# Four graph layers on one core: probabilities turned through scratch memory, columns spread by TensorE, one low part moved to GpSimd

## The reference

```python
def layer0(x):   # scores from two products
    e = leaky_relu((x @ W1) @ (x @ W2).T, 0.2)
    return relu(softmax(where(adj > 0, e, -inf)) @ (x @ W3))

def gat(x, W, a, masked):   # layer 1 is elu(...) of this, masked
    h = x @ W
    e = leaky_relu((h @ a1)[:, None] + (h @ a2)[None, :], 0.2)
    return softmax(where(adj > 0, e, -inf) if masked else e) @ h

def layer2(x):   # the "mixed" layer
    o = relu(x @ mlp1 + b1)                             # 512 wide
    o = elu(elu(gat(relu(o), W_fc, a_fc, False))) + o
    o = relu(o @ mlp2 + b2)                             # 256 wide
    return relu(elu(elu(gat(o, W_hand, a_hand, True))) + o)

def layer3(x):   # masked attention, 4 heads of 64, output product with wo
    ...
```

## Time and profile before

| | |
|---|---|
| median of 3 runs | 2919.27 us (2908.69 to 2920.22) |
| the profiled execution | 2918.28 us, its span 2916.5 us |
| TensorE busy | 2689.4 us, 92% |
| VectorE, ScalarE, GpSimd busy | 2278.2, 1998.7, 1556.0 us |
| mean granted TensorE clock | 0.983 of full speed |
| DMA | 195.17 MB, mean 67 GB/s |

### The profile page before, as it was taken

One profiled execution on the slowest core, in us unless ns is written; L12 is line 12 of the kernel. 1 busy time (PEld: TensorE's weight loads), 2 busy tenths in 40 slices (PEclk: granted clock), 3 DMA queues, 4 the chain that ended last, 5 costly groups with the idle time before them and its releaser, 6 DMA issues.

```text
span 2916.5 us, 61536 instructions
## 1 busy us (share of the span) xinstructions
PE 2689.4 (92%) x22472; PEld 2551.3 (87%) x22472; DVE 2278.2 (78%) x6124; ACT 1998.7 (69%) x4801; POOL 1556.0 (53%) x2119
## 2 busy tenths in 40 slices
PE   4689999999999999999999999999999999999974
PEld 4589999999999999998999998999999999998863
DVE  3257888888888888888888887888888888888874
ACT  1357777777777776777777777777777777776752
POOL 0235555555555555555556555555655555555542
PEclk9799999999999999999999999999999999999997
DMA  3001222222122122212212221221222122122222
GB/s 109 19 16 37 77 81 64 57 81 80 41 80 81 59 63 80 74 47 81 80 51 71 81 72 49 81 81 48 74 81 70 52 80 80 41 81 73 66 66 73
DMA packets 132766, 195.17 MB, mean 67 GB/s; under 512 B 14832, under 2 KB 97136, under 8 KB 132464
## 3 DMA queue, kind: packets, MB, share of 16 engines
q1 hardware_dynamic: 132464, 191.24, 22.7%
HBM read 107.30 MB, written 83.89 MB: 66 GB/s over the span
## 4 chain that ended last, share of the span: by engine, by line
PE 60%; DMA 13%; ACT 8%; SPq 8%; DVE 6%; issue 4%; POOL 1%; POOLq 0%; DVEq 0%
PE ps L224 29%; DMA p4T<-scratch 10%; PE ps L378 6%; SPq L208 6%; PE ps L240 5%; PE ps L436 4%; PE ps L337 4%; PE ps L233 3%; PE ps L338 3%; DMA scratch<-p 3%; DVE p L950 3%; PE ps L456 2%; ACT p L671 2%; PE ps L360 2%; DVE h_lo L692 1%
## 5 line engine op out<-in xcount | busy, mean ns | idle before, releaser
L1067 POOL TENSOR_TENSOR p<-p,rd 128x512 f32<-128x512 f32 x256 | 269.8, 1054 | 20.0
L671 ACT ACTIVATE p<-p,nmx 128x256 f32<-128x256 f32 x512 | 255.7, 504 | 25.4 <-DVE nmx L935 25.2
L991 POOL TENSOR_TENSOR o1Tp_lo<-o1T,o1Tp_hi 128x1024 fp32r<-128x1024 f32 x64 | 153.8, 2403 | 220.8 <-ACT o1Tp_hi L472 220.8
L1003 POOL TENSOR_SCALAR xn<-act,nmean,rstd 128x256 f32<-128x256 f32 x384 | 243.6, 643 | 18.3 <-POOL rstd L998 11.2
L456 PE MATMUL ps<-p4T,v 128*64 128x256 f32 x1024 | 144.3, 404 | 118.2 <-DMA p4T<-scratch 117.7
L995 POOL TENSOR_TENSOR vare<-mv,eps 128x2 f32<-128x2 f32 x256 | 108.0, 422 | 270.5 <-DVE mv L748 270.5
L1060 POOL TENSOR_TENSOR rd<-some,den 128x2 f32<-128x2 f32 x256 | 53.5, 209 | 354.6 <-DVE den L944 354.6
L456 PEld LDWEIGHTS ps<-p4T,v 128*64 128x64 f32 x1024 | 67.3, 140 | 178.1 <-DMA p4T<-scratch 96.5
L692 DVE TENSOR_TENSOR xnT_lo<-ps,xnT_hi 128x512 fp32r<-128x512 f32 x192 | 132.1, 688 | 114.2 <-ACT xnT_hi L472 114.2
L935 DVE CUSTOM_DVE_ANT_0 p<-ps,mask 128x256 f32<-128x256 f32 x512 | 189.9, 418 | 33.3 <-PE ps L436 33.3
L480 ACT ACTIVATE sco<-sco,nmax 128x256 f32<-128x256 f32 x384 | 191.0, 500 | 28.9 <-DVE nmax L736 28.9
(11 more groups left out here) (248 smaller groups left out, 12683.1 us busy)
## 6 DMA issues: line engine op xcount, KB each, us to landing
scratch<-p SPq DMA_DIRECT2D x128, 512.0 KB, 2.9
p4T<-scratch SPq DMA_DIRECT2D x512, 128.0 KB, 3.9
x0T<-in_xT SPq DMA_DIRECT2D x64, 256.0 KB, 4.6
x<-in_x SPq DMA_DIRECT2D x64, 256.0 KB, 3.7
out<-xn SPq DMA_DIRECT2D x64, 256.0 KB, 3.0
o1T<-in_mlp SPq DMA_DIRECT2D x1, 512.0 KB, 4.4
p<-in_mlp SPq DMA_DIRECT2D x1, 512.0 KB, 4.5
att<-in_fc SPq DMA_DIRECT2D x1, 512.0 KB, 5.4
```

The lines of the kernel that those rows point to most:

```text
L671: ins = nc.scalar.activation(rows_, rows_, ACT.Exp, scale=-1.0, bias=nmx4[:, h, m:m + 1], accum_out=den4[:, h, m:m + 1])
L991: return G.tensor_tensor(lo, whole, hi.bitcast(fp32), ALU.subtract)
L1003: ins = G.tensor_scalar(xn[:, m, :], y[:, m, :], nmean[i][:, m:m + 1], rstd[i][:, m:m + 1], ALU.add, ALU.mult)
L1067: G.tensor_tensor(rows_, rows_, rd4[:, h, :].unsqueeze(2).unsqueeze(3).broadcast_to([P, NT, QUADS, CT * QP]), ALU.mult).then_inc(S["p4n"], 1)
```

## The change

- The probabilities of layers 0, 1 and the mixed layer no longer pass through TensorE (`t0`, `t1`, `t3` of TensorE are gone). VectorE turns 32x32 blocks from `sco` into `act` (`turn`), SP sends them to scratch (`o0 o1 o3`) and fetches them back into `sco` (`i0 i1 i3`), ScalarE makes the high part from there and GpSimd the low part (`t0 t1 t3` of its string). The mixed layer's `o3T`, which is added to the output, goes the same way (`o5`, `i5`, buffer `o3r`) in place of TensorE's `o3`.
- The column sums of the mixed layer's first attention come from four products of 256 columns with a 128x128 tile of ones, so that every partition holds them. VectorE makes the reciprocal of 128x256 from PSUM straight into `rdb`; `b2` on TensorE and its copy are gone.
- The low part of `o2T` (the input of `mlp2`) is made by GpSimd (`z2`) and no longer by VectorE; so is the last layer's norm (`n4`).
- Scores of layers 1 and 2 are written to `sco` in SBUF and no longer in place in PSUM, `ef` to `pfc`. Layer 0's product with the probabilities has bank 2, layer 1's bank 3; `enter` now guards each bank by itself. `xnT` has two buffers for three uses, `xn3` one; `x0T` lies in the place of its own low part, `pfc` too.
- Weights are loaded and split in four groups. Only the first (with `adj`) stands ahead of the first sample; `before` in `run` puts the rest of the set-up ahead of the steps that need it.
- All five order strings are new.

```diff
-    "sp": "lt:0 o40:7 st:9 o42:7 lx:1 i40:7 i42:7",
+    "sp": "i42:8 o5:6 o1:3 lt:0 i1:3 o0:1 i5:6 o3:6 st:8 i0:1 i3:6 o40:7 lx:1 o42:7 i40:7",
-    "pe": "h3:8 a0:3 v4:9 f3:8 x0:5 g0:2 s40:9 d2:7 x1:6 t3:8 s42:9 v2:7 a3:8 m2:6 h0:2 b2:7 n2:6 o3:8 w2:7 s0:2 h1:5 c2:6 f1:5 t0:2 a4:9 r2:6 t1:5 x3:8 y4:9 m3:7 n3:7 a1:5 f2:6 q4:8 k4:8",
+    "pe": "g0:0 c2:4 a1:3 h1:2 r2:4 a3:6 a0:1 f2:4 f1:2 a4:7 m3:5 y4:7 x1:3 h0:0 x3:6 m2:3 s0:0 q4:6 k4:6 h3:5 n2:3 v4:6 f3:5 d2:4 s40:6 v2:4 w2:4 s42:6 x0:1",
+    "ac": "h0:1 x3:7 p1:3 x2:5 q4:7 m2:4 s0:1 k4:7 h3:6 p0:1 n2:4 l0:0 u3:6 o2:4 p3:6 p40:7 t1:3 p41:7 y2:5 x0:2 p42:7 p43:7 k2:5 c2:4 a1:3 t0:1 t3:6 h1:2 z2:5 r2:4 a3:6 b3:6 g0:0 a0:1 u1:2 a4:7 f2:4 m3:5 o3:5 x1:3 w2:4",
+    "dv": "e3:6 s40:7 s41:7 t3:6 p40:7 v2:5 s42:7 p41:7 s43:7 n2:5 x0:2 p42:7 i2:5 p43:7 x40:7 c2:4 x42:7 b1:3 j2:5 a1:3 h1:2 i3:6 r2:4 c3:6 st1:3 i0:1 b3:6 a3:6 ag1:3 r3:6 f2:4 z3:6 a4:7 st3:6 ag3:6 g0:0 b2:4 y4:7 o3:5 x1:3 e1:2 h0:0 x3:6 st4:7 st0:1 ag4:7 t1:2 ag0:1 i1:2 q4:6 e0:0 k4:6 h3:5 t0:0 v4:6 d2:4",
+    "po": "v0:2 n4:8 w2:5 n0:2 l0:0 m2:4 d40:7 t1:3 p40:7 d41:7 p41:7 d42:7 p42:7 d43:7 p43:7 k4:7 t3:6 t0:1 y1:3 z2:5 v1:3 n1:3 v3:6 n3:6 a0:1 m3:5 v4:7",
...
+            def pro_out(i):
+
+                def step(t):
+                    sp.wait_ge(S[f"pro{i}_x"], t + 1)
+                    wait(sp, S[f"pro{i}_dma"], back(t - 1))
+                    sp.dma_start(scratch_pro[i].rearrange("p w n -> p (w n)"), flat(act[i])).then_inc(S[f"pro{i}_dma"], 16)
+                return step
+
+            def pro_in(i):
+
+                def step(t):
+                    sp.wait_ge(S[f"pro{i}_dma"], sent(t))
+                    rows_ = sco[i][:, :, :, :].rearrange("p b a n -> p (b a n)").rearrange("p (q n) -> p q n", q=QUADS)
+                    for w in range(QUADS):
+                        sp.dma_start(rows_[w * QP:(w + 1) * QP, :, :], scratch_pro[i][:, w, :].rearrange("(q j) n -> j q n", q=QUADS)).then_inc(S[f"pro{i}_dma"], 16)
+                return step
...
             def d2(t):
+
                 pe.wait_ge(S["pfcl"], t + 1)
-                for m in range(NT):
-                    for k in range(NT):
-                        for i in (1, 0):
-                            ins = nc.tensor.matmul(ps[:, 5, 2 * m:2 * m + 2], pfcp[i][:, k, m * P:(m + 1) * P], ones2[:, :],
-                                                   start=(k == 0 and i == 1), stop=(k == NT - 1 and i == 0))
+                enter(5, "rdb", t + 1)
+                for k in range(NT):
+                    for i in (1, 0):
+                        ins = nc.tensor.matmul(ps[:, 5, 0:N], ones2[:, :], pfcp[i][:, k, :], start=(k == 0 and i == 1), stop=(k == NT - 1 and i == 0))
                 ins.then_inc(S["d2_mm"], 1)
...
             def d2(t):
                 dv.wait_ge(S["d2_mm"], t + 1)
-                V.reciprocal(rdc[:, :], ps[:, 5, 0:4:2]).then_inc(S["rdc"], 1)
+                wait(dv, S["att"], t)
+                V.reciprocal(rdb[:, :], ps[:, 5, 0:N]).then_inc(S["rdb"], 1)
...
+            def turn(i):
+
+                blocks = sco[i][:, :, :, :].rearrange("p b a n -> p (b a) n").rearrange("p c (w j) -> p w c j", w=QUADS)
+                return V.transpose(flat(act[i]).rearrange("p (w c j) -> p w c j", w=QUADS, j=QP), blocks)
...
             def t0(t):
-                dv.wait_ge(S["proT0h"], t + 1)
-                low_part(proT[0], bank[0]).then_inc(S["proT0"], 1)
+                dv.wait_ge(S["pro0"], t + 1)
+                wait(dv, S["xn0"], t)
+                turn(0).then_inc(S["pro0_x"], 1)
...
+            def z2(t):
+                po.wait_ge(S["o2Th"], t + 1)
+                low_part(o2T[1][:, :, :], att[:, :, :], o2T[0][:, :, :]).then_inc(S["o2T"], 1)
...
+            def low_of_turned(pair, i):
+                source = sco[i][:, :, :, :].rearrange("p b a n -> p (b a n)").rearrange("p (q c i) -> p c q i", q=QUADS, i=QP)
+                lo, hi = (flat(h).rearrange("p (c q i) -> p c q i", q=QUADS, i=QP) for h in (pair[1], pair[0]))
+                return low_part(lo, source, hi)
```

More of the change, by code:

```diff
@@ L18, in parse, with run @@
     return [(name, int(stage)) for name, stage in (x.split(":") for x in text.split())]
-def run(engine, steps, B):
+def run(engine, steps, B, before={}):
     order = parse(ORDERS[engine])
@@ L27, in run @@
             if 0 <= k - s < B:
+                if k == s and name in before:
+                    before[name]()
                 steps[name](k - s)
@@ L163, in by_quads, with by_tiles, flat, sent @@
             return row.rearrange("p (b w j) -> p w b j", b=CT, w=QUADS)
+        def by_tiles(row):
+            return row.rearrange("p (b n) -> p b n", b=CT)
+        def flat(tile):
+            return tile[:, :, :].rearrange("p a n -> p (a n)")
+        def sent(t, n=QUADS):
+            return 16 * (n + 1) * t + 16
+        def back(t, n=QUADS):
+            return 16 * (n + 1) * (t + 1)
         def wait(eng, sem, n):
@@ L375, in mlp2 @@
[L375 to L380 removed]
+                pe.wait_ge(S["pfcl"], t + 1)
+                enter(5, "att", t + 1)
+                product3(half_of(5), hfc, pfcp, NT, 2, off=2).then_inc(S["w2_mm"], 1)
@@ L475, in leaky, with high_of_turned, graph_scores, renew @@
                 return nc.scalar.activation(dst, src, ACT.Prelu, bias=bias, alpha=SLOPE)
+            def high_of_turned(pair, i):
+                source = sco[i][:, :, :, :].rearrange("p b a n -> p (b a n)").rearrange("p (q c i) -> p c q i", q=QUADS, i=QP)
+                return copy(flat(pair[0]).rearrange("p (c q i) -> p c q i", q=QUADS, i=QP), source)
             def exps(i):
                 for m in range(NT):
-                    ins = nc.scalar.activation(sco[i][:, m, :], sco[i][:, m, :], ACT.Exp, scale=-1.0, bias=nmax[i][:, m:m + 1], accum_out=den[i][:, m:m + 1])
+                    ins = nc.scalar.activation(sco[i][:, :, m, :], sco[i][:, :, m, :], ACT.Exp, scale=-1.0, bias=nmax[i][:, m:m + 1], accum_out=den[i][:, m:m + 1])
                 return ins
-            def graph_scores(b, i):
-                leaky(ps[:, b, N:2 * N], ps[:, b, 0:N], cols[i][:, 0, 0:1])
-                return leaky(ps[:, b, 0:N], ps[:, b, 0:N], cols[i][:, 1, 0:1])
-            ac.wait_ge(S["made"], 1)
+            def graph_scores(tile, i):
+                for m in range(NT):
+                    ins = leaky(tile[:, :, m, :], by_tiles(ps[:, 1, 0:N]), cols[i][:, m, 0:1])
+                return ins
+            readers = []
+            def renew(read, n):
+                if readers:
+                    ac.wait_ge(S[readers[0]], readers[1])
+                readers[:] = [read, n]
             def l0(t):
@@ L718, in _, with split @@
-            dv.wait_ge(S["setup_pool"], 1)
-            V.tensor_copy(ones2[:, :], ones[:, :])
+            count = {"wsplit": 0}
+            def split(places):
+                for pair, rows_, cols_, whole in places:
+                    ins = V.tensor_copy(pair[0][:, rows_, cols_], whole)
+                ins.then_inc(S["wsplit"], 1)
+                count["wsplit"] += 1
+                dv.wait_ge(S["wsplit"], count["wsplit"])
+                for pair, rows_, cols_, whole in places:
+                    ins = V.tensor_tensor(pair[1][:, rows_, cols_], whole, pair[0][:, rows_, cols_].bitcast(fp32), ALU.subtract)
+                return ins
@@ L895, in r3 @@
             def r3(t):
-                dv.wait_ge(S["on3_mm"], t + 1)
+                dv.wait_ge(S["o3_dma"], back(t))
                 dv.wait_ge(S["q3"], t + 1)
-                V.tensor_tensor(act[2][:, :, :], act[2][:, :, :], bank[2], ALU.add).then_inc(S["r3"], 1)
+                for m in range(NT):
+                    row = act[2][:, m, :].rearrange("p (k q c) -> p k q c", k=CT, q=QUADS)
+                    ins = V.tensor_tensor(row, row, o3r[:, :, :, m, :].rearrange("p q k c -> p k q c"), ALU.add)
+                ins.then_inc(S["r3"], 1)
             def z3(t):
```

518 lines of the change are left out of this document (292 added, 226 removed), and 3 rows, old and new, of the table ORDERS.

## The result

The changed kernel takes 3025.04 us (median of 4 runs, 3024.26 to 3029.68) against 2916.61 us of the kernel before on the same chip: ratio 1.0362, 95% interval 1.0335 to 1.0389. It is slower; the forecast was 2817 us, faster, with a range that ended at 2910.

What follows compares the result with a forecast made beforehand. The round was taken as a loop of PE segment A plus stretch L, 23.4 + 17.9 = 41.3 us. Then 245 + 63 x 41.3 - 47 + 15 = 2815, with 1.8 around it 2817 us; range 2690 to 2910.

Steps and rivals of the forecast that it cites:

- PE's work: TensorE's work a round: 41.05 us less 2.48 for removed turns, spread and cheaper `d2`, so 38.6.
- L: Stretch from the end of `s42` until `p4T` is there for `a4`: 18.6 us before, forecast 17.9.
- A: PE segment from second half of `a4` to end of `s42`, without a gap: 24.1 us before, forecast 23.4.
- the line on the masks of layers 1 and 2: VectorE's masks reading scores from SBUF: extra cost between nothing and 0.97 us each, taken as 0.
- The reciprocal: VectorE's pass over 128x256 from PSUM: taken at 0.45 us, between 0.43 and 1.4.
- slack on PE is 0.8 us: Claim that `s40` on PE, with `d2` running just ahead of its masks, has 0.8 us to spare.
- The rival: VectorE and GpSimd block each other, adding 1.0 in L and 2.0 in A: round 44.3, 3004 us; chance 13%.
- the forecast's own signs: Forecast wrong if PE waits inside A, POOL or SP queue chain shares rise well, or two-source passes grow 0.5 each.
- DVE's sum: VectorE's busy time a round: 35.19 us before, forecast 34.2, hidden below the round of 41.3.
- Start and end: Ramp and drain: first product at 13 us instead of 45.16, `a4` first passing at 245, end 15 after last `a4`.
- The drain: End of the run: saves 47 us against full rounds, as in the kernel before, and stays so.
- The sum: Whole time: 245 + 63 x 41.3 - 47 + 15 = 2815, with 1.8 us around the span 2817.

Runs made afterwards that it cites:

- all cures: Changed kernel plus scores of layers 1 and 2 in PSUM, `z2` on VectorE, `o1Tp_lo` in halves, `a1` ahead of `j2`: 2841.45 us, ratio 0.9758.
- e3: Not a run: a step in VectorE's string, two masks over 128x256, ahead of `s40` and `s41`; no time of a kernel belongs to it.
- The swap: `a1` put ahead of `j2` in VectorE's string: 2854.24 us on PSUM scores with wide reciprocal; 2900.46 against 2925.81 with the old column sums.

## Why the prediction was wrong, step by step

- **PE's work, right.** 38.6 a round forecast, 39.03 measured.
- **L, right in its sum, by luck in its parts.** From the end of `s42` (1469.74) to the second half of `a4` (about 1486.9, which no longer waited) it is at most 17.2; forecast 17.9. `a3`'s wait of 1.78 for VectorE lies in it, so the path through `p4T` is not what set it there. With all cures, where `p4T` is waited for, L is 17.6. But `x42` ends 9.0 after `s42` in the changed kernel and 8.8 with all cures (1435.6), not 7.9 to 8.2: GpSimd's last product with the reciprocals ends at 7.7 (1477.47) and not 6.7, and its small step `rd` over 128x2 takes 0.54 on average and up to 1.18, 0.21 before, as in the meetings with VectorE. And from there to `p4T` it takes 8.8, not the 9.7 that were to stay, since the DMA out took 3.29 and not 3.94, the last one in 4.18 and not 4.40. Two errors of nearly a microsecond cancel. SP's 20 more issues did not delay `o42` or `i42` beyond that: the three issues between out and in still take 1.3 us.
- **A, wrong, and with it the sign.** Forecast 23.4; measured 27.2 (1442.5 to 1469.74). PE's waits inside it in this round are 0.54 (`m3`), 1.00 (`s0`), 0.29 (`s40` for `v`) and 1.83 (`s42`), 3.7 together. The forecast had none of them. With all cures 0.46 (for `nmax`) and 0.30 (`s40` for `v`) are left, and A is 24.2.
- **The step that failed** is the line on the masks of layers 1 and 2: "lower bound unchanged, upper 0.97 more for each", and "I take 0, since PE doesn't wait on them now". The measured cost is 0.79 for each, four a round. That PE did not wait on them in the kernel before said nothing of the new string, in which they stand between two products of PE: `e1` ahead of `h0` and `s0`, `e3` ahead of the masks for which `s42` waits. The upper bound (0.97) was near the mark; taking the lower one was the error. The run with the scores in PSUM gave 5.2% back, more than the whole 3.6% of loss.
- **The reciprocal, mis-sized.** Taken at 0.45 with an upper bound of 1.4; measured 1.757, outside the bound. The bound came from the difference of two rows with two elements a partition (0.15 and 0.14), too small a difference to give the time of an element. With "slack on PE is 0.8 us" this is 1.3 us of work over 0.8 of slack. It is shown by the run without the division: 4.6%. With the masks cured it costs 0.4 to 0.6% (2864.93 to 2852.29, 2841.45 to 2828.95).
- **Both together.** One loop explains why the two did not add. `d2` on PE, the reciprocal, `e3`'s masks, those of `s40` and `s41`, `s42`: either cure takes `s42`'s wait of 1.83 away, and a further cut finds the next loop. A shorter reciprocal also moves the masks off GpSimd's pass (1212 to 789 ns), which is how 1.3 us of pass can give 2.2. The masks in PSUM take `s0`'s wait for `h_lo` (1.00) away too, hence 2.6 (44.46 to 41.87).
- **The second loop**, once the first is cured, is `a3` waiting for `a1` on DVE behind `j2` (1.5 to 1.8 us in the rounds read; `j2`'s `att<-ex,att` takes 2.31 beside GpSimd's turned low parts). The forecast had no wait for `a3`. The swap removes its row from the waits; it is worth 1.0% in one pair of kernels, 0.6% in another, and nothing certain once `z2` is back on DVE.
- **The rival was right.** "DVE and POOL block each other: slower" gave a round of 44.3 and 3004 us; measured 44.45 and 3025. Its place ("the `e1`, `h0`, `s0` sequence has no slack") was one of two; it had 2.0 us in A and 1.0 in L, and the changed kernel has 3.7 in A, the reciprocal's part included, and 1.78 for `a3` in L. So its total is close partly by luck. It had 13%; of the forecast's own signs, waits of PE for `h_lo` and `nmx` in A, POOL's share of the chain (12%, before 1%) and longer two-source passes all came. The trace had shown the lock in the earlier trace rows, and four passes had just been moved to the operands that lock. The two cited rules, on what excludes what and on turning tiles with TensorE (the Trainium skill, SBUF - State Buffer, "Who interferes with whom", and VectorE: DVE Perf Modes, "Rules for kernel authors"): the first agrees here, 2.40 us with both of a mask's sources in SBUF against 0.42 with one in PSUM; the second does not decide, since with the masks in PSUM the change as a whole gains 1.6 to 2.6%, and the turns were not tried apart from the rest.
- **DVE's sum.** Forecast 34.2, measured 40.05. The rows account for the 5.9: masks 4 x 0.79 = 3.2, reciprocal 1.3, `c3` 0.6 (mean 1.535, before 0.894), `att<-ex,att` 0.6 (2.013, before 1.446), `att<-att,o1T` 0.4 (1.580, before 1.228), 6.1 in all. POOL 31.8 forecast and 32.4 measured; ACT 31.2 at most and 30.4.
- **Start and end.** First product at 13.71 (forecast 13), first second half of `a4` at 239.75 (forecast 245). The drain, which was to save 47 us against full rounds as before, saves less, about 26: 63 x 44.46 less the 2775.1 from 239.75 to 3014.89. It was carried over from the kernel before without a reason, and was the largest of the small misses.
- **The sum, tested.** With every cure and the reciprocal at the forecast's price the kernel takes 2829 us in rounds of 41.22 (mean); the forecast was 2817 in rounds of 41.3. The sum's form holds for a kernel in which the two costs taken at nothing are in fact nothing, but not each term: A is 24.3 for 23.4, L 17.1 for 17.9. By the trace of that kernel the terms are 236.0 + 63 x 41.22 - 20.6 + 13.0 = 2825.3, its span: the start gives 9 us, the rounds 5, the end 2, and the drain, which saves 20.6 and not 47, takes 26. (The cures also change the kernel: `z2` is back on VectorE and GpSimd's `o1Tp_lo` is in halves.)

The best kernel found keeps the change and adds the PSUM scores, `z2` on DVE and `o1Tp_lo` in halves: 2841.43 us, ratio 0.9738. With the swap in place or without it, the times are the same within their intervals.

## What to carry to other kernels

A cost taken at nothing because PE does not wait on it now has to be looked up in the new order, not the old one: a pass that stands between two products of PE can be on the path. Where an operand moves from PSUM to SBUF while GpSimd gets more work, take GpSimd's longest pass as the upper price of each such pass, and count the places where the two meet rather than busy time. If two suspected costs stand one behind the other ahead of the same wait, cure both in one run as well as each alone: here 4.6% and 5.2% made 5.9%. Cutting the other engine's pass in halves helps a pass that stands alone (`c3`); where two such passes follow each other, as `e3`'s masks do, the second waits for the second half.

## What the runs showed of the hardware

- RECIPROCAL on VectorE over 128x256 from PSUM takes 1.757 us, a multiply and add of the same shape 0.424, RECIPROCAL over 128x2 0.15: about 6.3 ns an element more than the first few, (1.757 - 0.15)/254.
- The custom masking pass (two sources and a maximum) took from 0.36 to 2.40 us for 128x256 with both sources in SBUF, and never over 0.43 with one in PSUM, beside the same GpSimd work. In the two meetings shown the mask ended 0.28 us after GpSimd's pass (1466.84 and 1466.56; 1446.55 and 1446.27).
- A `tensor_scalar` with one source in SBUF over 128x512 also waits: 1.535 beside GpSimd's 2.4 us pass, 0.776 when that was cut in halves, 0.421 when it was gone.
- Both sides pay: `gT_lo` on GpSimd took 2.25 us behind DVE's `att<-ex,att` (1480.17 and 1478.98 in the changed kernel), against 1.29 for the same pass in rounds where they did not meet, and 1.28 for `x0Tp_lo` of the same shape.
